# Sigmoids, table loads and two output units in another place of ScalarE's order, for a bidirectional WKV scan with a binarised linear layer

## What is computed

```python
tf = sigmoid(sum(cond))[:, None, None]
decay = exp(-exp(w))[None, :] * (0.5 + 0.5 * tf[:, :, 0])
ek = exp(min(k, 30)); ekv = ek * k
# forward and backward in time, for (a, b): a = a * decay + ekv_t ; b = b * decay + ek_t
euk = exp(min(u + k, 30))
num = nf + nb - ekv + euk * k
den = df + db - ek + euk
r = sigmoid(x) * (num / max(den, 1e-8)) * (0.8 + 0.2 * tf)
bw = where(weight >= 0, 1, -1) * mean(abs(weight), axis=1)
out = x + einsum('bsi,oi->bso', r, bw) + bias
```

## Time and profile before

| | us |
|---|---|
| median of three runs | 514.83 |
| lowest, highest | 514.81, 516.65 |
| the profiled execution | 513.96 |
| its span in the trace | 512.1 |
| VectorE busy | 482.4 |
| ScalarE busy | 411.1 |
| GpSimd busy | 381.1 |
| TensorE busy | 354.7 |

### The profile page before, as it was taken

How to read it: one execution, slowest core, us unless ns; L and a number is a source line. 1 busy time by engine, 2 the same in 40 slices (tenths; PEclk the granted TensorE clock), 3 DMA queues, 4 the chain that set the end, 5 groups by cost and what they waited for, 6 DMA issues and landing times.

```text
span 512.1 us, 5399 instructions
## 1 busy us (share of the span) xinstructions
PE 354.7 (69%) x1803; PEld 209.6 (41%) x1803; DVE 482.4 (94%) x346; ACT 411.1 (80%) x459; POOL 381.1 (74%) x210
## 2 busy tenths in 40 slices
PE   3322223332288876877688698788849999999996
PEld 2212222332244443444254354355425555544442
DVE  6999998999999999999999999989999999999666
ACT  3978998898889879988988988898698888894500
POOL 0067769848777886888689678869778889999483
PEclk9996656555687998889898889979788999999999
DMA  8877999999997989598798957879866559995368
GB/s 216 228 213 241 256 224 234 293 314 242 265 245 188 204 194 165 142 200 190 161 199 190 205 83 209 162 164 206 165 114 90 108 102 150 193 153 78 42 113 217
DMA packets 101283, 94.22 MB, mean 184 GB/s; under 512 B 2924, under 2 KB 93064, under 8 KB 100744
## 3 DMA queue, kind: packets, MB, share of 16 engines
q0 software_dynamic: 31440, 36.18, 46.1%
q1 hardware_dynamic: 67720, 56.65, 35.1%
q10 hardware_dynamic: 2096, 1.05, 0.8%
HBM read 60.31 MB, written 37.75 MB: 191 GB/s over the span
## 4 chain that ended last, share of the span: by engine, by line
POOL 23%; ACT 23%; PE 22%; issue 16%; DVE 14%; DMA 0%; SPq 0%; DVEq 0%; ACTq 0%; POOLq 0%
POOL wkv L379 9%; PE prod L447 8%; DVE terms L925 4%; POOL acts L342 4%; DVE terms L911 4%; POOL wkv L385 4%; POOL out_dram L355 3%; PE prod L488 3%; ACT x_nat L796 3%; ACT rec L690 2%; ACT terms L655 2%; ACT euk L659 2%; ACT rec L692 2%; PE sT L488 2%; PE kT L488 2%
## 5 line engine op out<-in xcount | busy, mean ns | idle before, releaser
L447 PE MATMUL prod<-acts,sgn 128*128 128x512 f16 x752 | 180.2, 395 | 0.0
L925 DVE TENSOR_TENSOR_SCAN terms<-cols,y_start,terms 128x1024 f32<-128x1024 f32 x64 | 147.0, 2337 | 1.1
L911 DVE TENSOR_TENSOR_SCAN terms<-cols,terms 128x1024 f32<-128x1024 f32 x64 | 142.7, 2270 | 0.0
L447 PEld LDWEIGHTS prod<-acts,sgn 128*128 128x128 f16 x752 | 76.7, 102 | 86.6 <-issue 13.5
L362 POOL TENSOR_TENSOR wkv<-wkv,terms 128x1024 f32<-128x1024 f32 x31 | 73.4, 2367 | 50.7 <-DVE wkv L954 50.7
L379 POOL TENSOR_TENSOR wkv<-euk,rec 128x1024 f32<-128x1024 f32 x31 | 82.3, 2654 | 37.2 <-ACT rec L692 37.2
L385 POOL TENSOR_TENSOR wkv<-wkv,rec 128x1024 f32<-128x1024 f32 x31 | 81.8, 2639 | 1.2 <-ACT wkv L755 1.2
L342 POOL TENSOR_TENSOR acts<-wkv,rec 128x1024 f16<-128x1024 f32 x30 | 77.7, 2590 | 4.7 <-ACT rec L701 4.6
L422 PE MATMUL prod<-ident,o_nat 128*128 128x128 f16 x64 | 8.3, 311 | 72.8 <-ACT o_nat L790 72.8
L422 PE MATMUL kT<-ident,k_nat 128*128 128x128 f32 x248 | 45.9, 347 | 16.7 <-DVE own L942 16.5
L422 PE MATMUL sT<-ident,x_nat 128*128 128x128 f32 x208 | 38.0, 343 | 25.4 <-DVE wkv L954 16.7
(11 more groups left out here) (119 smaller groups left out, 587.0 us busy)
## 6 DMA issues: line engine op xcount, KB each, us to landing
terms<-own POOLq DMA_DIRECT2D x32, 512.0 KB, 5.2
out_dram<-in_x_dram SPq DMA_DIRECT2D x32, 512.0 KB, 7.2
k_nat<-in_fside_BxSxS_dram SPq DMA_DIRECT2D x30, 512.0 KB, 6.1
x_nat<-in_x_dram SPq DMA_DIRECT2D x26, 512.0 KB, 3.6
out_dram<-o_nat POOLq DMA_DIRECT2D x24, 512.0 KB, 8.0
y_fm<-in_L_ffn_weight_dram SPq DMA_DIRECT2D x8, 512.0 KB, 8.0
out_dram<-in_L_ffn_bias_dram POOLq DMA_DIRECT2D x8, 512.0 KB, 7.5
x_end<-in_x_dram SPq DMA_DIRECT2D x6, 512.0 KB, 8.9
```

Source lines behind the costliest of these rows:

```text
L447: ins = pe.matmul(made_in(u), view[:, c, m % CT * P:m % CT * P + P], acts[:, part, m // CT % 2 * CT + c, h * H:(h + 1) * H], start=(part = ...
L911: dve.tensor_tensor_scan(buf, d, buf, 0.0, ALU.mult, ALU.add).then_inc(st["F" + kind], 1)
L925: dve.tensor_tensor_scan(buf[:, ::-1], d, buf[:, ::-1], y_start[:, i:i + 1], ALU.mult, ALU.add)\
```

## The change

- **Turns.** A turn now happens in steps n % 3 == 2 below 26 (2, 5, ..., 23), and a short one with tiles 0 and 1 in step 0. In a turn step ScalarE loads the sigmoid set right behind the reciprocal, does the halves, the sigmoid of tile n, L755, the sigmoid of n+1, the relu of the next tile, the sigmoid of n+2, from step 8 on the one of a last tile, loads the other set back, and then takes the exponentials. `exps` is split into `below` (the relu) and `exps`.
- **Units in turn steps** all stand behind the exponentials.
- **Hasty steps**, which do the halves ahead of the first unit, are now n % 3 == 0 up to 24.
- **Sets one step sooner**: the six last tiles of x are loaded in steps 2 to 7, and their sigmoids taken in steps 8 to 23 instead of 9 to 24.
- **Unit 31** is evacuated in step 24, and its copy stands behind L755; on TensorE 12 matmuls of unit 34 go ahead of the transposes of unit 31.

```diff
--- before.py
+++ after.py
@@ -63,7 +63,7 @@
     def made(n):
         return 0 if n < LAG else 2 * LAST if n > N - 4 else MORE.get(n, 2 * (n - LAG + 1))
 
-    CLEARED = {23: 32, 25: 35, 26: 38, 27: 41, 28: 44, 29: 47}
+    CLEARED = {25: 35, 26: 38, 27: 41, 28: 44, 29: 47}
 
     def cleared(n):
         if n < LAG or n >= N - 2:
@@ -295,8 +295,8 @@
 
                     done(sp, "kT", n + 1)
                     sp.dma_start(k_nat[1 - p][:, :, :], tile_of(k, n + 3)).then_inc(k_in[1 - p], 16)
-                if 4 <= n < 10:
-                    sp.dma_start(x_of(SOON + n - 4), tile_of(x, SOON + n - 4)).then_inc(s_soon, 16)
+                if 2 <= n < 8:
+                    sp.dma_start(x_of(SOON + n - 2), tile_of(x, SOON + n - 2)).then_inc(s_soon, 16)
                 if n == N - 2:
 
                     done(sp, "sT", N - 4)
@@ -549,9 +549,9 @@
                 if sooner:
                     k_turn(n + 1, 1 - p)
                 if ahead:
+                    part(made(n) + 2, 0, CT - 2)
                     turned(made(n) - 1)
-                    for u in (made(n) + 1, made(n) + 2):
-                        part(u, 0, CT - 2)
+                    part(made(n) + 1, 0, CT - 2)
                     done(pe, "yc", made(n) - 1)
                     part(made(n), 0, CT - 2)
                     for u in range(made(n), made(n) + 3):
@@ -648,11 +648,14 @@
             act.wait_ge(s_every, 1)
             act.activation(ecs[:, :], csum_ps, ACT.Exp, scale=-1.0).then_inc(s_ecs, 1)
 
-            def exps(n, p):
+            def below(n, p):
 
                 done(act, "kT", n)
                 done(act, "den", n - 2)
                 act.activation(ek[p], kT[:, :], ACT.Relu, scale=-1.0, bias=cap[:, 0:1]).then_inc(st["below"], 1)
+
+            def exps(n, p):
+
                 act.wait_ge(s_capped, 1)
                 done(act, "below", n - 1)
                 act.activation(ek[p], ek[p], ACT.Exp, scale=-1.0, bias=capped[:, n:n + 1]).then_inc(st["expE"], 1)
@@ -728,8 +731,12 @@
                 if n == N - 1:
                     early_out(4)
                     early_out(5)
-                hasty = low and n < LAST and n % 3 == 1
-                if hasty:
+                turn = n % 3 == 2 and n < SOON
+                hasty = low and n <= LAST and n % 3 == 0
+                if turn:
+                    act.preload_act_table_set("sigmoid_and_others")
+                if hasty or turn and low:
+
                     done(act, "base", n - 2)
                     halves(n - 2, p)
                 sooner = cleared(n - 1) if n == LAST + 2 else min(made(n - 1), cleared(n - 1) + 1)
@@ -741,14 +748,16 @@
                         ins = act.activation(oscale[:, b * CT:(b + 1) * CT], asum[:, :], ACT.Identity,
                                              scale=gain[:, b:b + 1])
                     ins.then_inc(s_osc, 1)
-                if n == LAST:
-                    y_copy(4 * CT - 1)
-                if late and n < N - 2 and not hasty:
+                if late and n < N - 2 and not hasty and not turn:
                     clear(cleared(n - 1), sooner)
-                if low and not hasty:
+                if low and not hasty and not turn:
 
                     done(act, "base", n - 2)
                     halves(n - 2, p)
+                if turn:
+
+                    x_landed(act, n)
+                    act.activation(x_of(n), x_of(n), ACT.Sigmoid).then_inc(st["sig"], 1)
                 if mid:
 
                     done(act, "chk", n - 1)
@@ -756,6 +765,8 @@
                                    scale=-HI_SCALE * LO_GAIN, bias=2.0 * HI_SCALE * LO_GAIN).then_inc(st["two"], 1)
                 if late and hasty:
                     clear(cleared(n - 1), sooner)
+                if n == LAST:
+                    y_copy(4 * CT - 1)
                 if n == N - 2:
                     early_out(0)
                     y_copy(2 * LAST - 1)
@@ -765,8 +776,26 @@
                 if LAST + 1 < n < N - 2:
                     clear(sooner, min(sooner + 1, cleared(n)))
                     sooner += 1
+                if turn:
+
+                    x_landed(act, n + 1)
+                    act.activation(x_of(n + 1), x_of(n + 1), ACT.Sigmoid).then_inc(st["sig"], 1)
+                if nxt:
+                    below(n + 1, 1 - p)
+                if turn:
+                    if n + 2 < SOON:
+                        x_landed(act, n + 2)
+                        act.activation(x_of(n + 2), x_of(n + 2), ACT.Sigmoid).then_inc(st["sig"], 1)
+                    if n >= CT:
+
+                        act.wait_ge(s_soon, 16 * (N - SOON))
+                        i = SOON + (n - CT) // 3
+                        act.activation(x_of(i), x_of(i), ACT.Sigmoid).then_inc(st["soon"], 1)
+                    act.preload_act_table_set("natural_log_exp_and_others")
                 if nxt:
                     exps(n + 1, 1 - p)
+                if late and turn:
+                    clear(cleared(n - 1), sooner)
                 if n == N - 2:
                     for i in (1, 2, 3):
                         early_out(i)
@@ -789,16 +818,11 @@
                     done(act, "wT", n - 2)
                     act.activation(s_nat[p], w_nat[p][:, :], ACT.Sign, scale=TINY_GAIN, bias=tiny[:, 0:1])\
                        .then_inc(st["sgn"], 1)
-                if n % 3 == 0 and n < SOON:
-
-                    for i in range(n, min(n + 3, SOON)):
+                if n == 0:
+
+                    for i in range(2):
                         x_landed(act, i)
                         act.activation(x_of(i), x_of(i), ACT.Sigmoid).then_inc(st["sig"], 1)
-                    if n >= 9:
-
-                        act.wait_ge(s_soon, 16 * (N - SOON))
-                        i = SOON + n // 3 - 3
-                        act.activation(x_of(i), x_of(i), ACT.Sigmoid).then_inc(st["soon"], 1)
                     act.preload_act_table_set("natural_log_exp_and_others")
                 if wt:
```

## The result

The changed kernel takes 523.36 us (median of four runs, 520.68 to 523.79), the kernel before in the same session 515.16 (514.81 to 516.65). The ratio is 1.0143, 95% interval 1.0102 to 1.0183: **slower, by 7 to 8 us**. The forecast was 518.6 us, range 512.5 to 521.5. The direction held, the size did not, and the time lies outside the range. The profiled execution of the changed kernel took 523.79 us, its span is 521.8; before they were 513.96 and 512.1. It was the slowest of the four, so what it lost, 9.7 us of span, is somewhat more than the medians differ by (8.2 us). T(25), the waits and the span are always those of one profiled execution.

What follows compares the result with a forecast made beforehand. VectorE was taken to set the pace until 384.60 us, TensorE after it; losses to T(25) of 7.0 + 2.6 + 6.4 + 7.5 = 23.5 against 18.6, less 1.1 returned, gave 514.83 + 3.8, rounded to 518.6 us, range 512.5 to 521.5.

Steps and rivals of the forecast that it cites:

- The formula, loss = (start of L379 after T) - 4.8: Step loss from GpSimd's L379 starting late after T, VectorE's first product; 6.88 gave 2.07 us at step 19.
- The cover is 0.07 us: In turn steps, the exponential VectorE wants comes 13.85 us after T, just under the 13.92 of its next step.
- turns 11 and 14: Turns in steps 11 and 14 together cost 2.6 us where the trace before loses 4.1.
- Steps 2 to 10: Early steps, with a weight tile and ScalarE short of time: 7.0 us lost against 6.6 before, no gain.
- (d): Rival: third sigmoid of three or four turns waits 1 us for its x tile; about 522 us, chance 0.05.
- Turn 17: Step 17: late evacuation idles TensorE 8 us, 16 matmuls then take 5.5 to 6.3; loss 6.4 us.
- (c): Rival: TensorE's clock never falls behind the gap, turn in step 17 loses 4.0; 511.7 us, faster, chance 0.13.
- Turns 20 and 23: Steps 20 to 25: two turns at 1.3, TensorE's lag 3.3, VectorE's wait in step 25 1.6; sum 7.5 us.
- The wait by copy 31: Step 24's copy, behind TensorE's work, delays relu and exponential; VectorE waits 1.3 to 2.0 us in step 25, 1.6 taken.
- After 384.60 the end follows TensorE: Last stretch: the end follows TensorE's last big wait, ending 8.8 us after T(25) instead of 9.9; 1.1 us returned.
- (a): Rival: each table load inside the chain holds ScalarE another 1.28 us; +9.5, about 528 us, chance 0.03.
- (b): Rival: TensorE catches up in steps 21 to 25 as its clock returns sooner; 514.7 us, no change, chance 0.23.

Runs made afterwards that it cites:

- e8: The changed kernel with the second exponential of tiles 9, 12, 15, 18, 21 and 24 cut to half its columns; 520.58 us, ratio 1.0088.
- e2: The changed kernel with step 17's first unit cleared right behind the halves, ahead of the sigmoids; 517.14 us, ratio 1.0048.
- e10: The changed kernel with units of steps 17 and 20 cleared sooner, second sigmoids moved ahead, copy 31 behind the exponentials; 508.20 us, ratio 0.9866.
- e4: The changed kernel with each turn's second sigmoid right behind the first, ahead of ScalarE's product that waits for GpSimd; 519.06 us, ratio 1.0092.
- e3: The changed kernel with copy 31 of step 24 behind the exponentials of tile 25, not ahead; 518.98 us, ratio 1.0084.

## Why the prediction failed

By its own steps:

**The formula, loss = (start of L379 after T) - 4.8**: held. In step 18 of the changed kernel the reciprocal ends at 282.18 and L379 starts behind it at 282.27, 10.74 after T(18) = 271.53; that gives 5.94, and 5.95 was lost.

**"The cover is 0.07 us"**: this is the step that failed first. It costed "the exponential that VectorE wants" at 13.85 after T, against 13.92, and left the second one, at 14.8, off the path. VectorE's first product waits for both; the second at 14.8 is 0.9 late, and the trace shows waits of 0.97 to 1.06 in five steps. e8 shows that it is the second. In turns 11 and 14 the price came out nearly right all the same, 2.8 for 2.6, but by luck, through a wrong mechanism: a VectorE that waits 1 us is later by it, so the reciprocal behind is less late, and the collision cost only 0.3 instead of 1.3 (L379 starts at 190.33, 5.09 after T(12), which gives 0.29 by the formula; 0.32 was lost). Where lateness was already counted by a wait it added up: 2.75 at T(9) where 1.4 was forecast, and 1.06 at T(18), for which nothing was.

**Steps 2 to 10**: 9.1 for 7.0. Turn 2 was right (3.1 for 3.2). Turn 5 cost 3.2 for 2.4, of which 0.57 is the tile that rival (d) had; turn 8 cost 2.75 for 1.4: its first exponential ends at 141.27, 1.6 us behind T(8) + 13.92, and the second 1.0 later.

**Turn 17**: right in place, mechanism and nearly in size: an idle stretch of 8.99 us for 8, 6.58 us for 16 matmuls where 5.5 to 6.3 was taken, 5.95 for 6.4. e2 removes it. With the forecast's middle, 5.9 us of matmuls, the loss would have been 5.3 (5.9 - 0.62, an estimate from the five traces), so the nearness to 6.4 is in part this execution's clock. Rival (c), which rested on TensorE keeping its clock, fell by the granted 0.54.

**Turns 20 and 23**: 9.0 for 7.5. The lag that the prediction saw at step 22 came, as 2.88 at T(23) and 0.38 at T(22), for 3.3; e10 shows that it comes from the unit deferred in step 20. The wait by copy 31 was sized at 1.6 and measured 3.15 with a loss of 3.52: the copy waited 3.80 us for TensorE, and again the second exponential stood behind. The 2.6 us of matmuls that the prediction put ahead of the copy it had right (12 in 2.75), but the 16 matmuls before them took 6.18 us at a granted clock of 0.58.

**"After 384.60 the end follows TensorE"**: the second step that failed. TensorE's busy share of that stretch was read as its being the bound. It took 1.1 us off. TensorE's last big wait ended 6.8 us after T(25) and not 8.8, at 390.74, 6.1 us later than before, and the span grew by 9.7 all the same. The end follows T(31) by 53 us in every trace, so all that VectorE loses up to there arrives. With 27.9 for 23.5 and nothing returned, 3.8 becomes 9.3.

**Rivals**: (a) is out. The second load of step 17 stands at 267.95 and the exponential behind it starts at 269.25, 1.30 later, in the middle of the chain as well; the sigmoid ahead ends at 267.93. The Trainium skill's page "ScalarE: Activation LUTs", section What ACT_TABLE_LOAD costs, has a drain of the load's own length on top; this trace disagrees again. (b), TensorE catching up, did not happen at T(23) or T(25). (d) was taken as a rival of 0.05 and is a part of what happened, in one turn of eight, for 0.57 us in this trace and up to 2.87 in others. The range was built as if the rivals excluded each other; a missed wait in every turn and one late tile together lay above its upper end.

## What to carry to other kernels

Before a stretch is called covered, read in the code every semaphore that the covered instruction waits for, not only the operand that it is known by: here a margin of 0.07 us was worked out to the first of two, and the second was 0.9 us behind it. An engine that is 98% busy in the last stretch need not set its end; look for an instruction that every trace finds at the same distance from the end, and who releases it. Where TensorE comes out of a gap inside the chain, compare the granted clock of both traces before a difference is put down to an edit. When work is packed between two table loads, ask of each thing pushed behind them (an evacuation, a copy) who stands still for it: moving one evacuation ahead, one copy behind and one sigmoid into a wait turned +1.4% into -0.8%, and a second evacuation and the early turns taken back made it -2.2%.

## What was not expected of the hardware

A TensorE idle for 8.99 us came back at a granted clock of 0.54 and did 16 matmuls in 6.58 us instead of the 3.62 of the earlier trace rows; in the kernel before, 4.61 us of idleness were followed by 5.07 us for as many. The time behind such a gap is not settled by its length: in step 17 it was 5.08 us behind 8.59 us idle (e8) and 6.14 behind 6.39 (e4). In the changed kernel the lower clock held over nearly all of those 6.58 us, and 3.7 us later (282.39) it was full again.

The transfer of one x tile, issued at the same place of the program in every execution, took 8.8 us in one and 11.1 in another (the change and e3), against a median of 4.4 and 4.0 for all of them.
